# A graph network in one program: the dense product of the message layers for 1792 nodes in four passes, with 24 to 38 of its steps moved ahead of the layer

## The reference, cut to what matters

```python
def sage_conv(x, src, dst, pW, pb, lW, lb, rW):
    msg = jax.nn.relu(x @ pW + pb)[src]
    agg = jax.ops.segment_sum(msg, dst, num_segments=N)
    deg = jax.ops.segment_sum(jnp.ones((src.shape[0],), msg.dtype), dst, num_segments=N)
    mean = agg / jnp.maximum(deg, 1.0)[:, None]
    out = mean @ lW + lb + x @ rW
    nrm = jnp.maximum(jnp.linalg.norm(out, axis=-1, keepdims=True), EPS_NORM)
    return out / nrm

x = x + attention(relu(layernorm(x)), ...)
h = relu(layernorm(x))
h = silu(sage_conv(h, ...)); h = silu(sage_conv(h, ...)); h = sage_conv(h, ...)
x = x + (layernorm(h) * ln_w + ln_b)
```

## Time and profile before

| | |
|---|---|
| three runs | 4392.05, 4396.35, 4418.06 us; median 4396.35 us |
| the profiled execution | 4385.32 us, span 4383.0 us, mean granted clock 0.799 |
| attention, first gather to last cell | 117.6 to 1611.8 us |
| layers, first gathers of the three | 1681.35, 2576.92 and 3474.6 us; last gather of all 4330.92 us |
| busy over the span | PE 70%, POOL 61%, PEld 39%, DVE 36%, ACT 23% |
| DMA | 723.53 MB, mean 165 GB/s |

### The profile page before, as it was taken

How to read it: one execution, slowest core, us unless ns; L and a number is a source line. 1 busy time by engine, 2 the same in 40 slices (tenths; PEclk the granted TensorE clock), 3 DMA queues, 4 the chain that set the end, 5 groups by cost and what they waited for, 6 DMA issues and landing times. The chain is left out here.

```text
span 4383.0 us, 42516 instructions
## 1 busy us (share of the span) xinstructions
PE 3067.8 (70%) x12268; PEld 1730.8 (39%) x12268; DVE 1563.8 (36%) x5471; ACT 1022.4 (23%) x2518; POOL 2672.0 (61%) x2800
## 2 busy tenths in 40 slices
PE   7378888767777754777887657778777656666664
PEld 4366667545555532333333323333333222222222
DVE  5166766434444432122222221232222312433434
ACT  4255555434443331011111110111111100000000
POOL 1466656666666644666666646666666466666663
PEclk9588888877777667888888788888997878888875
DMA  6477878544444414555555435555554345555652
GB/s 189 140 250 244 264 247 253 157 130 136 139 142 131 139 54 137 170 168 172 170 177 176 123 121 160 175 170 175 173 179 132 122 153 178 185 185 178 184 155 71
DMA packets 444986, 723.53 MB, mean 165 GB/s; under 512 B 115842, under 2 KB 272019, under 8 KB 444752
## 3 DMA queue, kind: packets, MB, share of 16 engines
q0 software_dynamic: 130480, 353.90, 28.4%
q1 hardware_dynamic: 313888, 366.87, 26.1%
q10 hardware_dynamic: 384, 0.00, 0.0%
HBM read 625.47 MB, written 95.00 MB: 164 GB/s over the span
## 5 line engine op out<-in xcount | busy, mean ns | idle before, releaser
L1147 POOL DMA_INDIRECT ring<-message_table,src_index x1785 | 1697.4, 951 | 1022.7 <-issue 501.9
L559 POOL DMA_INDIRECT ring<-attention_table,src_index x784 | 757.8, 967 | 489.5 <-issue 211.6
L1212 PE MATMUL ps<-ring,attention_work 128*128 128x512 f32 x1764 | 921.5, 660 | 62.7 <-ACT attention_work L1479 29.2
L1704 PE MATMUL ps<-ring,one_hot 128*128 128x265 f32 x1568 | 599.7, 494 | 149.0 <-issue 147.8
L1212 PEld LDWEIGHTS ps<-ring,attention_work 128*128 128x128 f32 x1764 | 359.4, 214 | 452.7 <-issue 418.4
L1282 PE MATMUL ps<-ring,attention_work 128*32 128x256 f32 x3570 | 407.3, 441 | 138.9 <-issue 133.0
L1437 ACT ACTIVATE ring<-ps 128x256 f32<-128x256 f32 (+1 forms) x225 | 86.2, 383 | 1611.3 <-DMA attention_work<-run_flags 1448.6
L1352 DVE TENSOR_TENSOR attention_work<-attention_work,ps 128x160 f32<-128x160 f32 (+2 forms) x261 | 73.4, 294 | 1013.8 <-DMA root<-in_x 860.8
L1704 PEld LDWEIGHTS ps<-ring,one_hot 128*128 128x128 f32 x1568 | 337.3, 238 | 228.7 <-issue 197.7
L1224 PE MATMUL ps<-attention_work,ring 128*128 128x144 f32 x900 | 209.8, 366 | 311.0 <-ACT ring L1437 158.5
L1250 PE MATMUL ps<-w_l,attention_work 128*128 128x256 f32 x588 | 187.9, 449 | 234.5 <-issue 127.6
(11 more groups left out here) (167 smaller groups left out, 3071.9 us busy)
## 6 DMA issues: line engine op xcount, KB each, us to landing
ring<-dense_adjacency SPq DMA_DIRECT2D x441, 256.0 KB
attention_work<-message_table SPq DMA_DIRECT2D x441, 128.0 KB
attention_work<-in_dst_edges SPq DMA_DIRECT2D x112, 448.0 KB
dense_adjacency<-root SPq DMA_DIRECT2D x49, 768.0 KB
ring<-message_table,src_index POOLq DMA_INDIRECT x1785
attention_sums<-sums_out SPq DMA_DIRECT2D x112, 132.5 KB
ring<-attention_table,src_index POOLq DMA_INDIRECT x784
message_table<-attention_work SPq DMA_DIRECT2D x98, 128.0 KB
```

The costliest lines, as they stand in the source:

```text
L559: pool.indirect_dma_start(m.ring[:, k, t, 0:cols], None, table, bass.IndirectOffsetOnAxis(ap=m.src[:, at:at + 1], axis=0)).then_inc(s[f"ro ...
L1147: pool.indirect_dma_start(m.quad_ring[:, k, j, :], None, m.tables[w.l], bass.IndirectOffsetOnAxis(ap=m.src[:, t:t + 1], axis=0)).then_inc( ...
L1212: last = nc.tensor.matmul(m.ps[:, 2 + half, :], m.m_rows[:, k, half * P:(half + 1) * P], m.a_rows[:, k, :], start=(j == 0), stop=(j == BLO ...
L1704: last = nc.tensor.matmul(m.ps[:, 6 + parity, 0:SUMC], m.one_hot[:, parity, t, :], m.ring[:, k, t, 0:SUMC], start=(t == 0), stop=(c == 0 a ...
```

## The change

DENSE goes from 1536 to 1792, in passes of 256, 512, 512 and 512 destinations; a step of the first pass has matmuls of 256 columns. This makes 196 steps in a layer in place of 147. FIRST_TILE goes from 187 to 219 and WORK from 75 to 71 chunks (563 gathers a layer, 595 before), OWN from 197 to 229 cells, of which LATE_CELLS = 44 come after the last gather (32 before). `steps_done` now spreads columns, not steps. In layers 1 and 2, 38 steps are done before chunk 0: 24 of them in chunks 61 to 70 of the layer before, 14 after its last block. A stream of the first pass waits for the store of its own block, and the blocks of every pass are taken in the order in which they are stored. Zeros go out in two pieces of 896 columns in place of three of 512.

```diff
-DENSE = 1536
-HALF = 512
-PASSES = DENSE // HALF
+PASS_COLS = [256, 512, 512, 512]
+PASSES = len(PASS_COLS)
+PASS_AT = [sum(PASS_COLS[:part]) for part in range(PASSES)]
+DENSE, HALF = sum(PASS_COLS), max(PASS_COLS)
...
-COUNT_ROOT = 36
-ZEROS = 512
+COUNT_ROOT = 34
+ZEROS = 896
...
-ZERO_FROM, BUILD_FROM, LATE_CELLS = 1, 60, 32
+ZERO_FROM, BUILD_FROM, LATE_CELLS = 1, 60, 44
...
-DENSE_EARLY = 6
-DENSE_LAST = 64
-def steps_done(q):
-    if q >= DENSE_LAST:
+DENSE_EARLY, DENSE_AHEAD, DENSE_RESUMED = 6, 24, 38
+DENSE_LAST = 60
+def early_steps(l):
+    return DENSE_RESUMED if l else DENSE_EARLY
+def steps_done(q, l=0):
+    if q < DENSE_LAST:
+        early = cols_done(early_steps(l))
+        cols = early + (DENSE * BLOCKS - early) * (q + 1) // DENSE_LAST
+        return max(d for d in range(STEPS + 1) if cols_done(d) <= cols)
+    if l == LAYERS - 1:
         return STEPS
-    return DENSE_EARLY + (STEPS - DENSE_EARLY) * (q + 1) // DENSE_LAST
+    return STEPS + DENSE_AHEAD * (q - DENSE_LAST) // (WORK - 1 - DENSE_LAST)
...
             def stream(w, d):
                 u = w.step0 + d
-                k, j, half = u % STREAM, d % BLOCKS, d // BLOCKS
+                k, part, j = u % STREAM, d // BLOCKS, ORDER[d % BLOCKS]
+                if w.l and not part:
+                    stored = w.slot0 - BLOCKS + d
+                    sp.wait_ge(s[f"put{stored % 2}"], 16 * (stored // 2 + 1))
                 sp.wait_ge(s["streamed"].sem, s["streamed"].free(u))
...
-                table_done(sp, w.l)
-                while sent < STREAM:
-                    stream(w, sent)
-                    sent += 1
+                streams(early_steps(w.l) + STREAM if w.l else STREAM)
                 x1_in(w, 0)
...
-                    dense(steps_done(q))
+                    dense(steps_done(q, w.l))
```

More of the change, by code:

```diff
@@ L1005, with part_of, cols_done @@
 STEPS = PASSES * BLOCKS
-DENSE_EARLY = 6
-DENSE_LAST = 64
-def steps_done(q):
-    if q >= DENSE_LAST:
+DENSE_EARLY, DENSE_AHEAD, DENSE_RESUMED = 6, 24, 38
+DENSE_LAST = 60
+def part_of(col):
+    return max(part for part in range(PASSES) if PASS_AT[part] <= col)
+def cols_done(d):
+    part, some = divmod(d, BLOCKS)
+    return PASS_AT[part] * BLOCKS + some * PASS_COLS[part] if part < PASSES else DENSE * BLOCKS
+def early_steps(l):
[6 more added lines that the diff above has]
+    if l == LAYERS - 1:
         return STEPS
-    return DENSE_EARLY + (STEPS - DENSE_EARLY) * (q + 1) // DENSE_LAST
+    return STEPS + DENSE_AHEAD * (q - DENSE_LAST) // (WORK - 1 - DENSE_LAST)
 def node_slots():
@@ L1026, in node_slots @@
         q = min(q for q in range(WORK) if steps_done(q) >= (part + 1) * BLOCKS) + 2
-        for n in range(part * PASS_BLOCKS, (part + 1) * PASS_BLOCKS):
+        for n in range(PASS_AT[part] // P, (PASS_AT[part] + PASS_COLS[part]) // P):
             while q in taken:
@@ L1181, in _, with streams @@
             sp.dma_start(m.dst_at, m.at_dram).then_inc(s["places"], 16)
+            sent = 0
             for w in sweeps:
-                sent = 0
-                table_done(sp, w.l)
-                while sent < STREAM:
-                    stream(w, sent)
-                    sent += 1
+                def streams(end):
+                    nonlocal sent
+                    while sent < end:
+                        stream(w if sent < STEPS else sweeps[w.l + 1], sent % STEPS)
+                        sent += 1
+                streams(early_steps(w.l) + STREAM if w.l else STREAM)
                 x1_in(w, 0)
                 def chunk(q):
-                    nonlocal sent
                     i = w.slot_at(q)
-                    while sent < min(STEPS, steps_done(q - 1) + STREAM):
-                        stream(w, sent)
-                        sent += 1
+                    streams(min(steps_done(WORK - 1, w.l), steps_done(q - 1, w.l) + STREAM))
                     if i is not None:
@@ L1211, in sweep_step @@
                 for half in range(2):
-                    last = nc.tensor.matmul(m.ps[:, 2 + half, :], m.m_rows[:, k, half * P:(half + 1) * P], m.a_rows[:, k, :],
+                    last = nc.tensor.matmul(m.ps[:, 2 + half, 0:cols], m.m_rows[:, k, half * P:(half + 1) * P], m.a_rows[:, k, 0:cols],
                                             start=(j == 0), stop=(j == BLOCKS - 1))
@@ L1266, in second, with dense @@
                 project(w, i - 1)
+            done = 0
             for w in sweeps:
-                done = 0
-                while done < DENSE_EARLY:
-                    sweep_step(w, done)
-                    done += 1
+                def dense(end):
+                    nonlocal done
+                    while done < end:
+                        sweep_step(w if done < STEPS else sweeps[w.l + 1], done % STEPS)
+                        done += 1
+                dense(early_steps(w.l))
                 def chunk(q):
@@ L1285, in sums @@
                             last.then_inc(s["summed"].sem, 1)
-                    def dense(end):
-                        nonlocal done
-                        while done < end:
-                            sweep_step(w, done)
-                            done += 1
                     pe.wait_ge(s["onehot"].sem, s["onehot"].done(u))
@@ L1300, in chunk @@
                         turn(w, i - 1)
[L1301 removed]
+                        dense((done + steps_done(q, w.l) + 1) // 2)
                         combine(w, i, q)
[L1303 removed]
+                    dense(steps_done(q, w.l))
                     if i is not None:
@@ L1491, in chunk @@
                         second(w, i)
-                    if turns < PASSES and steps_done(q) >= (turns + 1) * BLOCKS:
+                    if turns < PASSES and steps_done(q, w.l) >= (turns + 1) * BLOCKS:
                         turn(w, turns)
```

20 lines of the change are left out of this document (11 added, 9 removed).

## The result

On the chip on which the kernel before had been timed, the changed kernel takes 4349.9 us (median of four, 4332 to 4356) against 4401.4 us (four, 4392 to 4418): ratio 0.988, 95% interval 0.985 to 0.991. That is 51 us less where 75 were forecast: within the 4282 to 4372 us given 8 in 10, above the forecast's own 4300 to 4340, and beyond what a measurement can miss. It lies only 2 us under the 4352 that I had set as the bound for a change that can be told. One of all the executions here, of the last experiment, ran in a slower state (4874.64 us at a granted clock of 0.547, its neighbours at 0.81) and is left out of its time.

The account below looks back on a forecast made before the run. The prediction took POOL's gathers plus a late release, 11.6 us a chunk, as the bound. Its terms, -139 + 27 + 15 + 20 + 0 + 2 = -75 us against 4396, gave 4320 us; own range 4300 to 4340, 8 in 10 for 4282 to 4372.

Parts of the forecast that it names:

- The gathers removed: Four chunks fewer in each of three layers, at 11.58 us a chunk: 139 us less.
- the lost cover: Added dense work in the layers' chunks, 0.6 to 1.4 us a chunk, was taken as hidden: zero loss.
- one more pass end: One more pass end in each layer, together with wider zeros and counting pieces in attention: 2 us more.
- the first rival: PE takes the lead in chunks with a block, so added dense work shows: 71 us, 4391 us in all; chance 12%.
- Cells: 20 more cells among the gathers of attention's chunks 60 to 111, 1.30 to 1.39 us each: 27 us more.
- Late cells: Twelve more cells after attention's last gather, 1.28 us each, delay the end of attention: 15 us more.
- the fourth rival: Late cells cost 0 and the last chunks' dense steps are half hidden: 4295 us; chance 12%.
- The transitions: Dense steps in a layer's last chunks, after POOL's last gather, are not hidden: 10 us at each of two, 20 more.
- The start of a layer: 14 narrow steps replace six before chunk 0, whose sums wait for the end of 40 gathers: 0 us.
- The third rival: Six stream buffers are too few for narrow steps: about 45 us lost, 4350 with half, 4365 with all; chance 13%.
- The working mechanism: While gathers run unbroken, PE's signals are seen late, about 1.6 us after a burst; a chunk costs 10.0 plus 1.6 us.

Follow-up runs that it names:

- the last experiment: The changed kernel taken further: dense product for 1920 nodes, 547 gathers a layer, 60 late cells; 4309.65 us, ratio 0.982 to the kernel before.
- cap: The changed kernel with one rule more: a chunk in which a pass ends does no step of the next pass; ratio 0.9879 to the kernel before.
- quads12: The changed kernel with a ring of six chunks of gathered rows in place of five; ratio 0.9934 to the kernel before.
- pause: The changed kernel with POOL waiting, before the gathers of chunks 1 to 4 of each layer, for the rows of the chunk before; 4357.6 us in one run.
- the fourth set: Runs on one chip with a pace of 10.0 us: kernel before 3707 us, changed kernel unchanged 3633.3 us, ratio 0.9806.
- the second: Set of runs on another chip with a pace of 10.0 us: kernel before 3701.2 us, changed kernel unchanged 3634.1 us, ratio 0.981.

## Why the prediction held, and where it was off

**The gathers removed** are the term that was mis-sized: 108 us among the gathers of the three layers in place of 139. The step that failed is the one that set the lost cover at zero, because chunks without dense steps were only 0.3 us faster. That reading gives the slope where PE has slack, and says nothing of where it ends. The other reading behind it, 1.7 us a chunk free because PE was busy for 85.5 of 100 us, took PE's rows for its work; where gathers run PE can be behind them, as SP's loads at the start of layer 1 show.

Layer 2 lost 4.5 us, layer 1 6 us, layer 0 20 us: the same order as the dense columns a chunk and the PE work beside them. The first two are 0.5 and 0.7% of a stretch read from one execution each and could be scatter; layer 0's 2.4% is not all scatter. That it is PE's work shows in the run with half of it left out: 17 us come back among the gathers of layer 0, 10 in layer 1, 2.4 in layer 2 (first to last gather 808.0, 806.5 and 803.6 us, with all of it 825.0, 816.8 and 806.0 us), some 30 us together. It leaves out about four times what the change added in layer 0 (134 us of PE work for 34), so it shows that PE's work costs time there, and not that the added part alone does.

The stop at the pass end, which I put into 2 us with "one more pass end", is 5 to 7 us of it. It is a mild form of the first rival, with a quarter to half of its 71 us. How much of layer 0's 20 us is scatter is open: with the same layer code it lasted 883.9 us in the profiled execution and 874.9 us on another chip of this kind, and chunks 41 to 58, with all the dense work and without the rule of `cap`, took 211.5, 209.1, 197.8 (`quads12`) and 199.8 us (`pause`), but 189.1 before the change.

**Cells**: the price was right. Attention's gathers took 32.8 us more in the profiled execution where I took 27 for 20 cells, but from chunk 60's first gather to the last it is 25 to 26 us more where the pace is 10.0 us (667.3 us before, 692.4 and 693.7 us after), and 1.31 us each in the run without them. The 32.8 is partly scatter: that stretch took 803.7 us there, and 789 to 799 us in the four other traces of this kind of chip with the same cells (771.5 us before). **Late cells** were right to 0.3 us and not hidden: the fourth rival is out. **The transitions** cost 14.5 and 6.6 us for a forecast of 10 and 10: the sum is right, the split is not. Halving the dense work takes 11 us off the first and nothing off the second, so that dense steps cause the 6.6 us is not shown. **The start of a layer**: first `keep` 56.6 us after the first gather in layers 1 and 2, 54 foreseen. In layer 0 it came at 48.0 us, and the second at 68.0, before which POOL stood for 8.3 us with its ring full. The third rival, too few stream buffers, cost next to nothing: from the first gather to that of chunk 6 it is 68.2 us in layer 0, for 67.9 us before the change, and from the `keep` of chunk 1 to that of chunk 20 it is 223.6 us for 219.6.

**The working mechanism** was right for the chip of the profile. Gathers in an unbroken row slow PE down, as the pause shows. It is not PE's load, as with half of the dense work the first `keep` of layer 1 still comes 56.2 us after the first gather; PE's order was not tried on such a chip. It was wrong as a statement about the kernel, since two of the four later sets show nothing of it. The Trainium skill, "SBUF — State Buffer", section "Who interferes with whom", says that DMA never contends with a compute engine. Where the pace is 10.0 us the trace agrees: `keep` 14.5 us after the first gather, with gathers running on. Where it is 11.6 us it doesn't: 56.6 us, and 22.1 us with a pause. There the measurement decides. The section speaks of memory ports, and that a port is what slows PE no run here shows.

**On the other kind of chip** the same sum gives 12 x 10.0 = 120 us less for gathers (measured 768.7 to 728.0, 768.6 to 727.0, 775.7 to 733.8 us, together 124), 26 us more for cells, 15 for the late ones, nothing for transitions: 79 us less. Measured are 67 and 74. The layers after are those of the fourth set; on the very chip of the layers before they took 729.2, 730.6 and 735.9 us, 117 us less together. What the forecast left out there is attention before its cells: from its first gather to that of chunk 60 it took 537.9 us before, 554.2 us after in the fourth set and 564.3 us in the second. Chunks 30 to 50 took 179.4 us before and 189.0 us after (fourth set), at a DMA share of 0.98 and 0.96:

```profile
391.40:570.80 179.40, 165.68 (x830) 134.47 (x830) 144.88 (x394) 124.41 (x288) 136.67 (x141) 0.93 0.98 310
```
```profile
386.20:575.20 189.00, 167.19 (x799) 133.21 (x798) 142.72 (x378) 119.54 (x276) 136.48 (x140) 0.90 0.96 309
```

In both the DMA engines are nearly full, at 310 and 309 GB/s, and the zeros and the tables for the counts move more bytes. On the first chip the added work was covered: the same chunks took 219.7 us before the change and 217.3 us after. Which of the two, zeros or counting, costs it was not tried.

## What to carry to other kernels

Before a slope is read as "covered", look for the place where the covering engine has least room and two of its costs meet in one chunk; the loss starts there and not evenly. An instruction on the engine that ends a stretch can be priced from one row: the late cells came out right to 0.3 us. What an engine's rows show can run ahead of what it has done; a wait on one of its early signals, here SP's loads, tells how far. A stall that no engine explains should be measured on a second chip before a mechanism of the kernel is made of it: here the same program took 4384 us on one and 3702 us on another.

## What the hardware showed that was not expected

- The same kernel runs at 11.6 us a chunk on some chips and at 10.0 us on others, with the same 0.95 us for a gather on POOL. The wait from POOL's last cell to the first gather of the layers is 70.6 us on one and 13.9 us on the other.
- On the slower kind, PE slows down from about 9 us into an unbroken row of indirect DMAs, by SP's loads; after 30 us it is at 2.8 us for each matmul row, whether a dense step has four of them or two. Its own rows show it some 20 to 30 us in. It recovers when the gathers end, and pauses of 2 to 7 us after each eight gathers keep it away for as long as they last. Why, and why on some chips only, stays open: the gathers' rows land on time in both as far as can be seen (PE's first sums are issued as soon as the dense steps are), and no engine's record shows a cause.
- The granted clock does not explain it: 0.87 in layer 0 of the changed kernel on the first chip, 0.94 on the other, both above the 0.80 of the half-dense run, which was faster than the first.
